# Flamingo gated block, one core: second output bank, earlier base weights, reordered K to Q change

## The chip, the cores and the metric

The kernel runs on one core of one Trainium2 chip. The metric is the device time of one execution in microseconds (us). Inputs are float32, and all matrix products are made from two-part splits: a value is rounded to a high part (a ScalarE copy to the fp32r type), the low part is value minus high part, and three matmuls (high by low, low by high, high by high) are summed. This is why nearly every operand passes ScalarE ("hi") and then VectorE or GpSimd ("lo") before TensorE may use it.

## What is computed

```python
# x (8,128,512), ctx (8,128,512), 32 heads of 128, mask per (batch, key)
def xattn(h):                                    # h = layernorm(x)
    q = (rmsnorm(h, ln_weight) @ w_q.T)          # (8,128,32*128)
    k, v = ctx @ w_k.T, ctx @ w_v.T
    s = softmax(where(m, q.k + position_bias, -inf)); s = where(m, s, 0)
    return h + (s @ v) @ w_out.T
def ffn(y):                                      # y = layernorm(x)
    base = y @ base_W.T + base_b                 # 512 x 512
    w = top-8 of softmax(y @ router_W.T + router_b), summed per expert by expert_map
    return base + 2 * sum_e w_e * (y @ A_e.T) @ B_e.T
x = x + tanh(g_xattn) * xattn(layernorm(x))
x = x + tanh(g_ffn) * ffn(layernorm(x))
```

## The kernel before

The program is written out by hand, one instruction stream per engine, with semaphores between them. It has three stages.

**K and Q.** 32 jobs (`JOBS`), job n for a pair of heads: jobs 0 to 15 make K from the context, jobs 16 to 31 make Q from the normalised x. `G` is 16, the number of the first Q job. From job 2 on, each job is a block-wise product with seven block multiplications m1 to m7 in place of eight (a Strassen-Winograd scheme). TensorE's order in a job is m1, m2, m4 of the job before, m6, m3 of the job before, m5, m7. The results R11, R21, R12, R22 are combined on VectorE (`c11`, `c12`, `c22`), rounded on ScalarE (`c11_hi`, `c21_hi`, ...), split on VectorE (`unit_lo`) and stored to `qk_units` in HBM. ScalarE also keeps copies of partial results (`snapshot_1` to `snapshot_3`, which write U1 to U3), on which m6, m7 and m4 wait. The weights of the next job are summed on VectorE (`weight_sums`, lines 930 to 935), rounded on ScalarE (`first_weights_hi`, `last_weights_hi`) and split on GpSimd. Beside this, jobs 3 to 13 normalise x (`layernorm_stats`, `rms_stats`, `norm_scales`, `normed`), and TensorE transposes it. At job 16 the four sums of x's blocks, T1 to T4, take the place of those of the context (`x_sum_hi`, `x_sum_lo`).

**Attention.** 64 units (`UNITS`): 8 groups of 4 heads by 8 batches. In step t each engine works on several units at once. TensorE: scores of unit t (line 1478), the two halves of V of unit t+1 (`v_half`), the two halves of the output product of unit t-4 (`out_half`), then probabilities times V of unit t-2 (`apply_probs`, line 1491). VectorE: adds the output of unit t-5 to `acc` (`add_out`, line 1082; in the last group `x1`, line 1095), V's low part, scores plus bias and mask and their maximum (lines 1048 to 1052), A's low part of unit t-3 (line 1056), then, when ScalarE has the exponentials (line 738), `rinv`, `rscale`, `p_norm` (lines 1060 to 1067) and a 32x32 block transpose (line 1073). SyncE sends the blocks to HBM (`p_rows`, line 333) and back transposed (`pT`, line 339), which ScalarE rounds two steps later (`probs_hi`) and GpSimd splits (`probs_lo`, line 516). GpSimd does four operations in a step: the rest of A (line 511), `probs_lo`, bias plus mask (line 504), and the low part of one weight tile.

**Last group and feed-forward.** In the last group (units 56 to 63) `x1`, the statistics and `y` of the second layernorm are added to VectorE's steps, and SyncE loads x again and the feed-forward weights. The base weights (`baseT`, 1 MB) go into the buffer `o_raw0`, which is free once output 55 is made (`o_done` at `LAST`). Then come the transposes of y, LoRA and router products, the base product and the result.

All outputs go to one PSUM bank, so an output waits for the sum of the one before it, which stands at the start of VectorE's step:

```python
# TensorE, out_half, first half
pe.wait_ge(a_lo_done, u + 1)
reached(pe, acc_done, u)          # last group: pe.wait_ge(f_x1, b)
# ScalarE, step, last group, ahead of exponentials(t)
if last and b >= 4:
    act.wait_ge(ld_base, 16)
    late_high(w_base_hi[:, b - 4, :], base_raw[:, b - 4, :])
```

## Time and profile before

| | |
|---|---|
| median of 3 runs | 892.32 us (890.05 to 893.9) |
| the profiled execution's own time | 891.21 us |
| its span, first to last instruction | 889.4 us |
| TensorE busy | 845.3 us (95%) |
| VectorE busy | 670.7 us (75%) |
| ScalarE, GpSimd busy | 499.1 us (56%), 487.3 us (55%) |
| mean granted TensorE clock | 0.984 |

The span is some 345 us of K and Q, some 455 us of attention up to the last group's units, and the rest. The busy shares are means over stages. A busy TensorE can still be one that follows another engine's pace with gaps of tenths of a microsecond, so the waits and the chain have to be read beside the shares. PE is TensorE, DVE is VectorE, ACT is ScalarE, POOL is GpSimd, SP is SyncE.

### The profile page before, as it was taken

Reading aid. Unit: us, or ns where it says so; the run is one execution under the profiler, and the core shown is the slowest. Engines: PE = TensorE matmul, PEld = TensorE weight load, DVE = VectorE, ACT = ScalarE, POOL = GpSimd, SP = SyncE. Lnnn points to the kernel's source line nnn. Section 1 sums busy time; section 2 is a strip of 40 time slices with the busy share of each in tenths; the row PEclk is TensorE's granted clock in tenths of the full one; section 3 lists DMA queues with packets and bytes.
Section 4 is the critical chain, followed back from the end, with each engine's and each line's share of the span. In section 5 each row is a group of like instructions: output and inputs, shape, how many; then the busy total and the mean of one; then the engine's idle time right before and its main releaser. Section 6 shows DMA issues by size and latency. Waiting matters only on the chain.

```text
span 889.4 us, 13885 instructions
## 1 busy us (share of the span) xinstructions
PE 845.3 (95%) x4204; PEld 706.6 (79%) x4204; DVE 670.7 (75%) x1174; ACT 499.1 (56%) x1185; POOL 487.3 (55%) x352
## 2 busy tenths in 40 slices
PE   6999999989999996999999999999999999977998
PEld 5877888768888884888888888888888888856786
DVE  6887777866766645888888888888888888859864
ACT  6556676666676643555555555655655555525310
POOL 0355334644466523666666666766666666646432
PEclk9999999999999998999999999999999999998999
DMA  8867677569877787889889898888888988974101
GB/s 289 307 238 284 258 263 280 205 261 356 301 272 279 274 314 236 249 242 259 235 239 259 239 256 248 249 261 244 241 255 250 253 252 248 272 214 133 46 25 71
DMA packets 155393, 214.73 MB, mean 241 GB/s; under 512 B 10960, under 2 KB 109392, under 8 KB 154960
## 3 DMA queue, kind: packets, MB, share of 16 engines
q1 hardware_dynamic: 155344, 214.13, 75.6%
q8 instruction: 24, 0.39, 0.2%
q14 instruction: 25, 0.20, 0.1%
HBM read 128.11 MB, written 85.98 MB: 241 GB/s over the span
## 4 chain that ended last, share of the span: by engine, by line
DVE 37%; PE 37%; ACT 12%; issue 7%; DMA 5%; DVEq 1%; SPq 1%; POOL 0%; ACTq 0%; POOLq 0%
ACT p_exp L738 10%; DVE p_norm L1067 6%; PE Sb L1331 5%; PE Sb L1333 5%; PE Sb L1332 5%; DVE s_sb L1050 4%; DVE negmax L1052 4%; DVE rscale L1062 4%; DVE V_lo L898 4%; DVE s_sb L1048 4%; DVE acc L1082 3%; PE Ab L1331 2%; PE Ab L1332 2%; PE Ab L1333 2%; DVE unit_out L898 2%
## 5 line engine op out<-in xcount | busy, mean ns | idle before, releaser
L467 POOL TENSOR_TENSOR w_lo<-w_raw,w_hi 128x1280 fp32r<-128x1280 f32 (+1 forms) x29 | 85.2, 2938 | 122.5 <-ACT w_hi L604 122.5
L511 POOL TENSOR_TENSOR a_rest<-small_a,A_hi 128x512 f32<-128x512 f32 x64 | 82.9, 1296 | 124.3 <-ACT small_a L732 124.2
L738 ACT ACTIVATE p_exp<-s_sb,negmax 128x128 f32<-128x128 f32 x256 | 99.8, 391 | 56.3 <-DVE negmax L1052 56.1
L1322 PE MATMUL Ob<-o_hi,A_lo 128*128 128x512 f32 x248 | 101.0, 407 | 17.5 <-DVE acc L1095 11.4
L516 POOL TENSOR_TENSOR P_hl<-pT,P_hl 128x512 fp32r<-128x512 f32 x64 | 83.0, 1297 | 39.5 <-ACT P_hl L604 39.0
L1323 PE MATMUL Ob<-o_lo,A_hi 128*128 128x512 f32 x248 | 98.2, 396 | 0.0
L1324 PE MATMUL Ob<-o_hi,A_hi 128*128 128x512 f32 x248 | 98.1, 396 | 0.0
L504 POOL TENSOR_TENSOR bm<-bias,maskneg 128x512 f32<-128x512 f32 x64 | 83.8, 1309 | 24.6 <-DVE s_sb L1048 24.6
L604 ACT ACTIVATE P_hl<-pT 128x512 fp32r<-128x512 f32 x64 | 40.5, 633 | 76.0 <-DMA pT<-p_rows 75.9
L604 ACT ACTIVATE U<-Sb 128x512 f32<-128x512 f32 x90 | 53.6, 599 | 47.1 <-PE Sb L1333 46.4
L604 ACT ACTIVATE A_hi<-Ab 128x512 fp32r<-128x512 f32 x64 | 38.4, 599 | 72.4 <-PE Ab L1492 72.4
L1322 PEld LDWEIGHTS Ob<-o_hi,A_lo 128*128 128x128 f32 x248 | 47.3, 191 | 38.4 <-issue 28.3
L604 ACT ACTIVATE w_hi<-w_raw 128x512 fp32r<-128x512 f32 (+2 forms) x67 | 60.1, 901 | 22.8 <-PE Kb L1333 7.3
L1060 DVE RECIPROCAL rinv<-rowsum 128x4 f32<-128x4 f32 x64 | 11.4, 178 | 80.8 <-ACT p_exp L738 80.8
L1331 PE MATMUL Sb<-t_hi,w_lo 128*128 128x512 f32 x180 | 70.3, 391 | 0.8 <-ACT U L604 0.7
L1491 PE MATMUL Ab<-P_hl,V_hi 128*128 128x256 f32 x256 | 63.7, 326 | 7.6 <-POOL P_hl L516 7.6
L1333 PE MATMUL Sb<-t_hi,w_hi 128*128 128x512 f32 x180 | 70.1, 389 | 0.0
L1332 PE MATMUL Sb<-t_lo,w_hi 128*128 128x512 f32 x180 | 70.0, 389 | 0.0
L1478 PE MATMUL Sb<-qk 128*128 128x256 f32 x256 | 66.4, 337 | 2.9 <-DVE s_sb L1050 2.2
L472 POOL TENSOR_TENSOR w_lo<-w_raw,w_hi 128x512 fp32r<-128x512 f32 x30 | 40.2, 1339 | 40.9 <-ACT w_hi L604 40.9
L898 DVE TENSOR_TENSOR unit_out<-Ob,unit_out 128x512 fp32r<-128x512 f32 x61 | 42.0, 689 | 23.7 <-ACT unit_out L604 23.0
L1491 PEld LDWEIGHTS Ab<-P_hl,V_hi 128*128 128x128 f32 x256 | 48.7, 190 | 11.1 <-POOL P_hl L516 8.7
(292 smaller groups left out, 2605.2 us busy)
## 6 DMA issues: line engine op xcount, KB each, us to landing
qk_units<-unit_out SPq DMA_DIRECT2D x128, 512.0 KB, 3.0
qk<-qk_units SPq DMA_DIRECT2D x64, 1024.0 KB, 7.2
p_rows<-p_blocks SPq DMA_DIRECT2D x64, 256.0 KB, 2.6
pT<-p_rows SPq DMA_DIRECT2D x256, 64.0 KB, 4.4
w_raw<-wqk SPq DMA_DIRECT2D x31, 512.0 KB, 4.3
v_raw<-wv SPq DMA_DIRECT2D x32, 256.0 KB, 4.8
o_raw<-wo SPq DMA_DIRECT2D x32, 256.0 KB, 5.0
stage<-ctxT SPq DMA_DIRECT2D x8, 256.0 KB, 6.2
```

Source lines behind the costliest of these rows:

```text
L467: pool.tensor_tensor(w_lo[:, n % 2, first:5, :], w_raw[:, n % 2, first:5, :], f32(w_hi[:, n % 2, first:5, :]), ALU.subtract).then_inc(w1_l ...
L504: pool.tensor_tensor(bm[:, :, :], bias4[:, q, :, :], maskneg[:, b:b + 1, :].broadcast_to([P, HU, S]), ALU.add).then_inc(bm_done, 1)
L604: act.activation(dst, src, ACT.Copy).then_inc(done, 1)
L738: last = act.activation(p_exp[:, i, :], s_sb[:, i, :], ACT.Exp, bias=negmax[:, i:i + 1], accum_out=rowsum[:, i:i + 1])
L898: dve.tensor_tensor(dst, src, f32(hi), ALU.subtract).then_inc(done, 1)
L1322: pe.matmul(dst, w_lo, m_hi, start=start, stop=False)
L1323: pe.matmul(dst, w_hi, m_lo, start=False, stop=False)
L1324: return pe.matmul(dst, w_hi, m_hi, start=False, stop=stop)
L1331: pe.matmul(bank, lo, m_hi[:, c, :], start=first, stop=False, skip_group_check=not fresh)
L1332: pe.matmul(bank, hi, m_lo[:, c, :], start=False, stop=False, skip_group_check=not fresh)
L1333: last = pe.matmul(bank, hi, m_hi[:, c, :], start=False, stop=c == 1, skip_group_check=not fresh)
L1491: pe.matmul(Ab[:, h, :, :], V_hi[:, r, h, :], P_hl[:, h, :, :], start=True, stop=False)
```

## The change

- Outputs of even batches go to `Ob`, of odd ones to `QP` (`o_bank`), so an output waits for the sum two before it. In the last group the banks are `Ob`, `QP`, `Ob`, `Vb`, `Ob`, `Vb`, `Ob`, `Vb`, and from the third batch on output b waits for `f_x1` at b-1 (the fourth for a V split instead). Two of the base product's banks are exchanged, and the first transpose of y waits for `f_x1` at 2.
- SyncE asks for the base weights at batch 3 of the last group instead of batch 4. ScalarE rounds three of their four tiles behind the exponentials of batches 5 to 7 and the fourth in the tail ahead of `probs_hi` of unit 62; GpSimd's splits follow (batches 5 to 7, and one in the tail).
- At job 16 VectorE makes R21's low part first, then R22's, then c11, and T4's low part behind it; ScalarE rounds R21 ahead of the next weights.
- x's statistics: the second half's four `bn_stats` are spread over jobs 4 to 7, its aggregates stand in job 7, its rms part in job 8 and its scale in job 9 (before: jobs 4, 5 and 6).
- Some semaphores are split: one for each weight tile of `wv` and `wo`, and one for each parity of the units for `pT`. No instruction is added by this.

The order of VectorE's instructions at job 16 (unit_out from Ob is R22's low part, from Sb R21's, from Vb R11's; lines 930 to 935 are the weight sums). Before, from the second sum of the weights:

```order
L935 TENSOR_TENSOR w_raw<-w_raw 128x256
L898 TENSOR_TENSOR t_lo<-stage,t_hi 128x1024
L898 TENSOR_TENSOR unit_out<-Ob,unit_out 128x4x128
L947 TENSOR_TENSOR Vb<-Ab,U 128x512
L898 TENSOR_TENSOR unit_out<-Vb,unit_out 128x4x128
L898 TENSOR_TENSOR unit_out<-Sb,unit_out 128x4x128
L959 TENSOR_TENSOR Ob<-Kb,U 128x512
```

Now (the code's lines have moved by 12):

```order
L947 TENSOR_TENSOR w_raw<-w_raw 128x256
L910 TENSOR_TENSOR unit_out<-Sb,unit_out 128x4x128
L910 TENSOR_TENSOR unit_out<-Ob,unit_out 128x4x128
L959 TENSOR_TENSOR Vb<-Ab,U 128x512
L910 TENSOR_TENSOR t_lo<-stage,t_hi 128x1024
L910 TENSOR_TENSOR unit_out<-Vb,unit_out 128x4x128
L971 TENSOR_TENSOR Ob<-Kb,U 128x512
```

The low part of R21 moved from the fifth place to the second, ahead of T4's low part (t_lo), and T4's now stands between c11 and R11's.

ScalarE in the last group, batch 4 before (o_hi from o_raw with ld_base is the first base tile):

```order
L604 ACTIVATE A_hi<-Ab 128x512 [waits o_done,pv_done]
L604 ACTIVATE V_hi<-Vb 128x512 [waits pv_done,v_done]
L732 ACTIVATE small_a<-Ab 128x512 [waits a_rest_done]
L604 ACTIVATE P_hl<-pT 128x4x128 [waits pv_done,pt_done]
L604 ACTIVATE o_hi<-o_raw 128x512 [waits ld_base]
L738 ACTIVATE p_exp,rowsum<-s_sb,negmax 128x128 [waits norm_done,max_done]
L738 ACTIVATE p_exp,rowsum<-s_sb,negmax 128x128 x3
```

Now, batch 5:

```order
L612 ACTIVATE A_hi<-Ab 128x512 [waits o_done,pv_done]
L612 ACTIVATE V_hi<-Kb 128x512 [waits pv_done,v_done]
L740 ACTIVATE small_a<-Ab 128x512 [waits a_rest_done]
L612 ACTIVATE P_hl<-pT 128x4x128 [waits pv_done,pt_done1]
L746 ACTIVATE p_exp,rowsum<-s_sb,negmax 128x128 [waits norm_done,max_done]
L746 ACTIVATE p_exp,rowsum<-s_sb,negmax 128x128 x3
L612 ACTIVATE o_hi<-o_raw 128x512 [waits ld_base]
```

The base tile moved from ahead of a unit's exponentials to behind those of the next unit.

SyncE's transfers in the last group, before, batches 3 end, 4 and 5 begin:

```order
L347 DMA qk<-qk_units 128x8x256 [waits scores_done]
L339 DMA pT<-p_rows 32x4x128 [waits rows_done]
L339 DMA pT<-p_rows 32x4x128 x3
L430 DMA x_again<-x 128x512 [waits f_u]
L433 DMA o_raw<-baseT 128x2048 [waits o_done]
L333 DMA p_rows<-p_blocks 128x512 [waits blocks_done]
L347 DMA qk<-qk_units 128x8x256 [waits scores_done]
L339 DMA pT<-p_rows 32x4x128 [waits rows_done]
```

Now:

```order
L346 DMA pT<-p_rows 32x4x128 [waits rows_done]
L346 DMA pT<-p_rows 32x4x128 x3
L437 DMA x_again<-x 128x512 [waits f_u]
L440 DMA o_raw<-baseT 128x2048 [waits o_done]
L340 DMA p_rows<-p_blocks 128x512 [waits blocks_done]
L354 DMA qk<-qk_units 128x8x256 [waits scores_done]
L346 DMA pT<-p_rows 32x4x128 [waits rows_done]
L346 DMA pT<-p_rows 32x4x128 x3
```

The base weights moved ahead by one round of probabilities, scores' operands and x.

The diff, without the semaphores that are split:

```diff
+        def o_bank(b):
+            return (Ob[:, :], QP[:, :])[b % 2]
...
-        out_bank = [Ob[:, :]] * 4 + [Vb[:, :], Ob[:, :], Vb[:, :], Ob[:, :]]
+        out_bank = [Ob[:, :], QP[:, :], Ob[:, :], Vb[:, :], Ob[:, :], Vb[:, :], Ob[:, :], Vb[:, :]]
...
-        base_bank = [flat(Ab)[:, 0:D], flat(Ab)[:, D:2 * D], Vb[:, :], Ob[:, :]]
+        base_bank = [flat(Ab)[:, 0:D], flat(Ab)[:, D:2 * D], Ob[:, :], Vb[:, :]]
...
-                    if last and b == 4:
+                    if last and b == 3:
                         sp.wait_ge(o_done, LAST)
                         sp.dma_start(base_raw[:, :, :], baseT).then_inc(ld_base, 16)
...
-                if last and b >= 4:
-                    late_low(b - 2, w_base_lo[:, b - 4, :], base_raw[:, b - 4, :], w_base_hi[:, b - 4, :])
+                if last and b >= 5:
+                    late_low(b - 3, w_base_lo[:, b - 5, :], base_raw[:, b - 5, :], w_base_hi[:, b - 5, :])
...
-                if n in (4, 5):
-                    rms_root(n - 4)
-                if n in (3, 4):
-                    layernorm_root(n - 3)
+                if n in (4, 8):
+                    rms_root(n // 8)
+                if n in (3, 7):
+                    layernorm_root(n // 7)
...
             late_root(3)
+            late_low(5, w_base_lo[:, 3, :], base_raw[:, 3, :], w_base_hi[:, 3, :])
             a_remainder(UNITS - 2, 0)
...
-                if last and b >= 4:
+                exponentials(t)
+                if last and b >= 5:
                     act.wait_ge(ld_base, 16)
-                    late_high(w_base_hi[:, b - 4, :], base_raw[:, b - 4, :])
-                exponentials(t)
+                    late_high(w_base_hi[:, b - 5, :], base_raw[:, b - 5, :])
...
+                if n == G:
+                    c21_hi(n - 1)
                 if n + 1 < JOBS:
                     first_weights_hi(n + 1)
...
-                if n > PLAIN:
+                if n > PLAIN and n != G:
                     c21_hi(n - 1)
...
             y_hi(0)
-            probs_hi(UNITS - 2, 0)
+            late_high(w_base_hi[:, 3, :], base_raw[:, 3, :])
+            probs_hi(UNITS - 2, 0, UNITS // 2)
...
-                dve.tensor_tensor(acc[:, b, :], Ob[:, :], acc[:, b, :], ALU.add).then_inc(acc_done, 1)
+                dve.tensor_tensor(acc[:, b, :], o_bank(b), acc[:, b, :], ALU.add).then_inc(acc_done, 1)
...
                 if n == G:
-                    x_sum_lo(T4)
+                    unit_lo(R21, n - 1, X[(n - 1) % 2])
                 if n > PLAIN:
                     unit_lo(R22, n - 1, C22)
                 c11(n)
+                if n == G:
+                    x_sum_lo(T4)
                 unit_lo(R11, n, C11)
-                if n > PLAIN:
+                if n > PLAIN and n != G:
                     unit_lo(R21, n - 1, X[(n - 1) % 2])
...
                 if n == 4:
                     rms_stats(0)
-                    layernorm_stats(1)
+                    tile_stats(1, 0)
                 if n == 5:
                     norm_scales(0)
+                if 5 <= n < 8:
+                    tile_stats(1, n - 4)
+                if n == 7:
+                    layernorm_stats(1)
+                if n == 8:
                     rms_stats(1)
-                if n == 6:
+                if n == 9:
                     norm_scales(1)
...
-                    if late and b == 4:
+                    if isinstance(u, int) and u == 1:
+                        pe.wait_ge(v_lo_done, 2)
+                    if late and b == 3:
                         pe.wait_ge(v_lo_done, UNITS - 1)
-                    elif late and b > 4:
+                    elif late and b > 1:
                         pe.wait_ge(f_x1, b - 1)
-                    elif late and b > 0:
-                        pe.wait_ge(f_x1, b)
                     else:
-                        reached(pe, acc_done, u)
+                        reached(pe, acc_done, u - 1)
...
-                if j < 2:
-                    pe.wait_ge(v_lo_done, UNITS if j == 1 else 2)
+                if j == 0:
+                    pe.wait_ge(f_x1, 2)
+                elif j == 1:
+                    pe.wait_ge(v_lo_done, UNITS)
                 else:
```

## Rows read from the trace of the kernel before

**Rows 1.** The page's chain of waits, by engine.

```profile
DVE 37%; PE 37%; ACT 12%; issue 7%; DMA 5%; DVEq 1%; SPq 1%; POOL 0%; ACTq 0%; POOLq 0%
```

**Rows 2.** The chain in order of time, one unit of attention: start us, us, what.

```profile
402.07 0.65 DVE acc L1082
...
405.39 1.66 ACT p_exp L738 x8
...
410.10 0.65 DVE acc L1082
```

**Rows 3.** VectorE's lines between 371 and 792 us: ns min/median/max, first and last start.

```profile
L1082 DVE TENSOR_TENSOR acc<-Ob,acc x56: 650/652/654, 372.2 to 786.3; 128x512 f32<-128x512 f32 x56
...
L1062 DVE TENSOR_TENSOR rscale<-rinv,valid x55: 161/590/1258, 377.4 to 784.7; 128x4 f32<-128x4 f32 x55
...
L1067 DVE TENSOR_TENSOR p_norm<-p_exp,rscale x56: 691/692/1737, 370.8 to 784.9; 128x512 f32<-128x512 f32 x56
```

**Rows 4.** Waits between 371 and 792 us: us in total, times, longest.

```profile
PE Ob L1322 <- DVE acc L1082: 5.4, 12, 1.3
```

**Rows 5.** Timeline, TensorE: start us, us, instruction [idle before it <-releaser].

```profile
785.36 0.33 PE L1478 MATMUL Sb<-qk 128*128 128x256 f32 x1
...
792.68 0.33 PE L1478 MATMUL Sb<-qk 128*128 128x256 f32 x1
...
803.44 0.76 PE L1322 MATMUL Ob<-o_hi,A_lo 128*128 128x512 f32 x1 [8.23 <-DVE acc L1095]
...
832.46 0.36 PE L1491 MATMUL Ab<-P_hl,V_hi 128*128 128x256 f32 x1 [0.73 <-POOL P_hl L516]
```

**Rows 6.** Timeline, last group: SyncE's transfers, ScalarE, VectorE, GpSimd.

```profile
786.38 0.34 SPq L333 DMA_DIRECT2D p_rows<-p_blocks  x1
...
791.58 0.43 SPq L433 DMA_DIRECT2D o_raw<-baseT  x1
...
788.21 0.63 ACT L604 ACTIVATE P_hl<-pT 128x512 fp32r<-128x512 f32 x1 [1.07 <-DMA pT<-p_rows]
798.61 0.63 ACT L604 ACTIVATE o_hi<-o_raw 128x512 fp32r<-128x512 f32 x1 [9.77 <-DMA o_raw<-baseT]
...
825.25 0.40 ACT L738 ACTIVATE p_exp<-s_sb,negmax 128x128 f32<-128x128 f32 x1 [5.12 <-DVE negmax L1052]
...
828.51 0.60 ACT L604 ACTIVATE A_hi<-Ab 128x512 fp32r<-128x512 f32 x1 [1.61 <-PE Ab L1492]
...
788.88 0.69 DVE L1052 TENSOR_REDUCE negmax<-s_sb 128x4 f32<-128x512 f32 x1
...
802.58 0.71 DVE L1095 SCALAR_TENSOR_TENSOR acc<-Ob,tgate,acc 128x512 f32<-128x512 f32 x1
...
830.98 1.28 POOL L516 TENSOR_TENSOR P_hl<-pT,P_hl 128x512 fp32r<-128x512 f32 x1
```

**Rows 7.** Transfers by line: KB each, median us from issue to landing.

```profile
p_rows<-p_blocks SPq DMA_DIRECT2D x64, 256.0 KB, 2.6
pT<-p_rows SPq DMA_DIRECT2D x256, 64.0 KB, 4.4
...
o_raw<-baseT SPq DMA_DIRECT2D x1, 1024.0 KB, 7.0
```

**Rows 8.** Timeline, K to Q change: TensorE, then VectorE, then ScalarE.

```profile
182.19 0.77 PE L1331 MATMUL Sb<-x_hi,w_lo 128*128 128x512 f32 x1 [4.10 <-DVE unit_out L898]
...
186.54 0.39 PE L1331 MATMUL Sb<-t_hi,w_lo 128*128 128x512 f32 x1
...
177.66 1.22 DVE L898 TENSOR_TENSOR t_lo<-stage,t_hi 128x1024 fp32r<-128x1024 f32 x1
...
183.17 0.59 ACT L604 ACTIVATE U<-Sb 128x512 f32<-128x512 f32 x1
```

**Rows 9.** Stretches: us, busy us of PE, PEld, DVE, ACT, POOL, then PEclk, DMA share, GB/s.

```profile
60.00:70.00 10.00, 8.62 (x40) 6.79 (x39) 8.09 (x17) 6.68 (x12) 6.44 (x5) 1.00 0.72 262
182.00:185.50 3.50, 3.31 (x8) 2.67 (x9) 2.70 (x7) 1.46 (x3) 1.07 (x1) 0.51 0.93 371
```

34 lines of the change are left out of this document (19 added, 15 removed).

## Prediction

> **What bounds the kernel now.** I read the page's shares first: TensorE 95% busy, VectorE 75%. That would make it a TensorE kernel. The chain of waits says otherwise: VectorE holds as much of it as TensorE (37% each) and ScalarE 12% [rows 1]. The chain in order of time shows where. In attention it runs from VectorE's sum into `acc` through its scores and maximum to ScalarE's exponentials (1.66 us) and back to VectorE, round and round, with no TensorE row in it; one such round took 410.10 - 402.07 = 8.03 us [rows 2]. So I took the pace: 56 sums into `acc` start from 372.2 to 786.3 us, which is 7.53 us a unit [rows 3]. TensorE, when nothing holds it, needs 792.68 - 785.36 = 7.32 [rows 5]. It follows. VectorE's round is long because two operations with both inputs in SBUF, `rscale` and `p_norm`, run between 161 and 1258 ns, and between 691 and 1737 ns [rows 3], with GpSimd at work beside them.
>
> Three places stand out against that pace. In batch 4 of the last group ScalarE waits 9.77 us for the base weights ahead of the exponentials, and TensorE's next output waits 8.23 us behind it [rows 5, 6]. At the K to Q change TensorE waits 4.10 us for VectorE [rows 8]. In the normalisation of x, TensorE is busy 8.62 us of 10 between 60 and 70 us [rows 9].
>
> **The base weights.** They are asked for at 791.58 us and ScalarE gets on at 798.61 [rows 6]. The transfer takes 7.0 us [rows 7]. Asked for a round earlier it is issued when output 55 is made, just ahead of step 60 at 785.36 [rows 5], 6 us earlier, and the first user is a unit later and behind its exponentials. Nobody waits for it. What is late next in batch 4 is VectorE's maximum (788.88 + 0.69 = 789.6; ScalarE is free at 788.8), so the exponentials start at 789.6 where they started some 0.5 after 798.61, at 799.2: 9.6 us. I take 0.4 off for `p_norm`, which then meets GpSimd; a meeting costs from 0 to 1737 - 691 = 1046 ns [rows 3]. x1 of batch 0 moves from 802.58 to 793.4 [rows 6], 9.2 earlier.
>
> From there to the end of the steps VectorE is the bound, and its shift holds. The exponentials of unit 63 come at 825.25 - 9.2 = 816.05 and end at 817.7. Before, ScalarE then waited 1.61 us for TensorE, which had been held by x1 [rows 6]; with its output bank free TensorE is early, and this wait goes. Ahead of the probabilities of unit 62 stand five conversions, two of them the moved base tiles, at 0.5 us from start to start (my estimate: they take 0.60 to 0.63 each and overlap a little [rows 6]), then 0.63 for itself: 820.8. GpSimd's split takes 1.28 [rows 6], so TensorE's product of unit 62 starts at 822.1 where it was 832.46 [rows 5]: 10.3 us. Behind it the tail is TensorE's own work nearly throughout, and the shift holds. The last base split on GpSimd (about 1.3 us) falls between a root and a wait for ScalarE; if that cover is gone it costs up to 1.3.
>
> The 1 MB is now under way when `p_rows` of unit 59 is issued (786.38), which takes 2.6 us by itself, and `pT` 4.4 [rows 6, 7]. Bounds: 0, if the earlier request only fills gaps; 4, if all of the probabilities of unit 59 stand behind it (the rival below). I take 0.5, nearer to 0, because they are read a step later. **Term: -9.8 us.**
>
> **The K to Q change.** R21's low part takes T4's place at 177.66 and is done at 178.3, so m1 of job 17 starts at 178.5 in place of 182.19. After m1 and m2 (2.7 us, below) m4 of job 16 wants to start at 181.2, but needs U3, which ScalarE ended at 183.17 + 0.59 [rows 8]. That copy follows c12, and only gains the 0.7 us in which VectorE waited between c11 and R11's split, now filled by T4. So m4 starts at 183.0 in place of 186.54 [rows 8]: -3.5 us, with an idle of 0.5 and one of 1.9 left. The granted clock was 0.51 in the 3.5 us from 182 us, after the idle of 4.10 us [rows 8, 9]; that is the level of 1.2 GHz. TensorE was busy 3.31 us of it, which would have been half at 2.4 GHz, so 1.65 us of the loss was clock, and m1 and m2, 186.54 - 182.19 = 4.35, need 2.7 at full rate. Bounds: -2.0, if it falls again after the smaller idles; -5.8, if U3 does not hold m4. **Term: -3.5 us.**
>
> **x's statistics.** The 1.38 us that TensorE loses there [rows 9] are two gaps of about the same length: one behind the four `bn_stats` and four aggregates of the second half, which goes, and one ahead of the first transpose, which still waits for the same operations. The aggregates land in jobs 7 and 8; VectorE was busy 8.09 us of 10 in this stretch [rows 9] and has room. **Term: -0.7 us**, between 0 and -1.4.
>
> **The two banks.** Removed is the wait of an output for the sum before it: 5.4 us in 12 waits [rows 4]. Against 7.32 a unit, TensorE is even (7.53 - 7.32) x 55 = 11.5 us over. I cost it at nothing. VectorE never waits for TensorE here, so a TensorE that runs further ahead changes no round; its waits come back at the next thing VectorE or the transfers give, the probabilities of unit t-2, some 0.6 us further on. Bounds: 0 and -11.5. In the last group the bank matters for the third and fourth output; that is in the 10.3. No added wait holds anything: the fourth output waits for the V split of unit 62, made a step before; output 60 needs x1 of batch 2, made at the start of step 63, ahead of A's low part for which it waits anyway.
>
> **Split semaphores** cost nothing: no instruction is added, and each wait is for the same data.
>
> **Sum**: -9.8 - 3.5 - 0.7 = -14.0. The profiled execution took 891.21 us (span 889.4), so 877.2. The median of the runs, 892.32, is 1.1 above it, and the runs spread over 3.9; I say 877.5.
>
> **Rivals.**
>
> *A, the two banks free attention.* If TensorE's lateness did reach VectorE, through the time at which GpSimd starts (it takes A's rest once TensorE's product is rounded), the pace falls towards 7.32 and up to 11.5 us more go: 866. For it: TensorE's outputs wait there 12 times. Against it: the chain has no TensorE row. 0.10.
>
> *B, the base weights hold the probabilities.* If transfers of a queue go one behind the other, 1 MB at the 262 to 371 GB/s of the stretches [rows 9] takes 2.8 to 4.0 us. `p_rows` then lands at 786.38 + 2.6 + 4.0 = 793, and `pT` 4.4 behind it, with its four issues at 797.4 to 799; ScalarE reads it ahead of exponentials that could start a round after 789.6, near 797.6, and GpSimd and TensorE follow. Cost 2 to 4: 880.5. For it: ScalarE waited for `pT` already 1.07 us in batch 4 [rows 6]. Against: the loads of scores' operands, as large, pass there in each round. 0.22. By the Trainium skill (DMA: Bandwidth & Descriptors, Queues, rings and completion order) descriptors are consumed in ring order on each DMA engine, which speaks for B; no row here shows the order.
>
> *C, slower: GpSimd meets VectorE in every unit.* TensorE ahead starts `a_rest` earlier, and so moves GpSimd's four operations against `rscale` and `p_norm`. In the worst rounds these cost 1.1 us more than their least (1258 - 161 [rows 3]), in the mean 0.6: the round of 8.03 had the 1.1 in it, 6.93 without, and the mean is 7.53. Were the worst to come in all 55 units, that is +0.5 x 55 = +27, net 905; it decides from +0.25 a unit on, a mean cost of 0.85. Against it: GpSimd's run starts with the probabilities, which come by transfers that VectorE paces, not TensorE. 0.03. The Trainium skill (SBUF — State Buffer, Who interferes with whom) has an exclusive lock between VectorE's operations with two SBUF inputs and GpSimd's; the spread there [rows 3] agrees. By it a shift of phase can turn the cost of a unit either way.
>
> *D, the K to Q change gains little*: the clock falls again and U3 holds m4, -2.0 or less; 879 with all else. 0.12.
>
> *E, nothing comes of it*: the wait of 9.77 us is replaced by one as long, say for scores' operands, whose load shares the queue. 887 to 890. 0.05.
>
> **How the numbers follow.** My forecast has 0.48, A 0.10, B 0.22, D 0.12, E 0.05, C 0.03. The range has to hold 8 in 10: B and D lie in it, half of A's way, and the run's own spread. 870 to 884. About 0.5% is what a measurement here can tell from no change, 4.5 us: faster means below 887.9. All but C and most of E are below: 0.92; within 0.5%: 0.05; slower: 0.03.
>
> **What the profile after would show.** Right: ScalarE's wait for `baseT` gone; TensorE without a wait over 3 us between 780 and 815; sums into `acc` still 7.5 us apart, and TensorE's waits in attention now at the probabilities (line of `P_hl`) instead of at the output; at 178 us an idle under 1 us and one near 2, for ScalarE's copy; full granted clock at both places. Wrong: a pace of 7.3 or of over 7.7 us in attention (A, C); a wait of ScalarE of over 3 us for `pT` in batch 5 (B); or a half clock after the small idles (D). The forecast falls if VectorE's steps in batches 5 to 7, where it is busy all the time, are longer than before.

## The result, and the profile after

The changed kernel takes 880.33 us (median of 4 runs, 876.11 to 884.0) where the kernel before takes 892.62 (4 runs). The ratio is 0.9856, with a 95% interval of 0.9814 to 0.9898. That is 12.9 us less, and between 9.1 and 16.6. The profiled execution was the slowest of the four, 884.0 us, span 882.1; its difference to the span before, 7.3 us, is smaller than the one between the medians. The table further down shows where these 7.3 us lie.

The page's chain of waits after, by engine (before: [rows 1]):

```profile
DVE 40%; PE 34%; ACT 12%; issue 7%; DMA 5%; SPq 1%; DVEq 1%; POOL 0%; ACTq 0%
```

VectorE's lines in attention after, 371 to 786 us (ns min/median/max, first and last start), against [rows 3]:

```profile
L1095 DVE TENSOR_TENSOR acc<-QP,acc x28: 650/652/654, 377.6 to 785.5; 128x512 f32<-128x512 f32 x28
...
L1075 DVE TENSOR_TENSOR rscale<-rinv,valid x55: 161/697/1312, 375.2 to 784.0; 128x4 f32<-128x4 f32 x55
L1080 DVE TENSOR_TENSOR p_norm<-p_exp,rscale x55: 691/692/1750, 376.3 to 784.2; 128x512 f32<-128x512 f32 x55
```

From the sum of output 1 (377.63) to that of output 55 (785.52) it is 407.9 us, 7.55 a unit: the pace is the old one, and `rscale` stalls as it did. Only the place of TensorE's waits has changed, from the output [rows 4] to the product with the probabilities, two thirds of it for A's low part and one third for the probabilities themselves (waits, TensorE, 371 to 786 us: us in total, times, longest):

```profile
PE Ab L1513 <- DVE A_lo L1069: 3.8, 9, 0.6
PE Ab L1513 <- POOL P_hl L523: 1.9, 4, 0.7
```

The K to Q change after, timeline: VectorE, then ScalarE, then TensorE, against [rows 8]:

```profile
177.53 0.68 DVE L910 TENSOR_TENSOR unit_out<-Sb,unit_out 128x512 fp32r<-128x512 f32 x1
...
182.76 1.08 ACT L612 ACTIVATE U<-Sb 128x512 f32<-128x512 f32 x2
...
178.36 0.47 PE L1353 MATMUL Sb<-x_hi,w_lo 128*128 128x512 f32 x1 [0.41 <-DVE unit_out L910]
...
183.50 0.47 PE L1353 MATMUL Sb<-t_hi,w_lo 128*128 128x512 f32 x1 [2.16 <-ACT U L612]
```

m1 of job 17 starts at 178.36 in place of 182.19, m4 of job 16 at 183.50 in place of 186.54, with the two idles that were forecast, 0.41 and 2.16. The windows that answer to [rows 9]:

```profile
60.00:70.00 10.00, 9.92 (x47) 7.98 (x46) 8.50 (x14) 6.02 (x10) 4.25 (x2) 1.00 0.68 257
182.00:185.50 3.50, 2.00 (x9) 1.71 (x10) 2.67 (x7) 2.18 (x4) 0.16 (x1) 1.00 0.87 349
```

The clock stays at full speed here, and the two gaps in the normalisation of x are gone, both of them. One of 0.39 us stands 10 us further on, ahead of the second tile's transposes, where there was none before:

```profile
78.16 0.66 PE L1447 MATMUL QP<-ident,xn 128*128 128x128 f32 x4 [0.39 <-DVE xn L1010]
```

The last group after: SyncE's transfers, ScalarE's waits, VectorE's first x1, and all that TensorE waits for from 780 us to product 63 ([rows 5, 6] before):

```profile
778.85 0.34 SPq L340 DMA_DIRECT2D p_rows<-p_blocks  x1
...
781.12 1.75 SPq L346 DMA_DIRECT2D pT<-p_rows  x4
...
783.38 0.43 SPq L440 DMA_DIRECT2D o_raw<-baseT  x1
785.63 0.33 SPq L340 DMA_DIRECT2D p_rows<-p_blocks  x1
...
791.34 2.75 SPq L346 DMA_DIRECT2D pT<-p_rows  x4
...
795.63 0.63 ACT L612 ACTIVATE P_hl<-pT 128x512 fp32r<-128x512 f32 x1 [2.67 <-DMA pT<-p_rows]
797.15 0.40 ACT L746 ACTIVATE p_exp<-s_sb,negmax 128x128 f32<-128x128 f32 x1 [0.88 <-DVE negmax L1065]
...
816.01 0.40 ACT L746 ACTIVATE p_exp<-s_sb,negmax 128x128 f32<-128x128 f32 x1 [3.79 <-DVE negmax L1065]
...
792.62 0.71 DVE L1108 SCALAR_TENSOR_TENSOR acc<-Ob,tgate,acc 128x512 f32<-128x512 f32 x1
...
782.89 0.36 PE L1513 MATMUL Ab<-P_hl,V_hi 128*128 128x256 f32 x1 [0.64 <-DVE A_lo L1069]
797.96 0.35 PE L1513 MATMUL Ab<-P_hl,V_hi 128*128 128x256 f32 x1 [0.17 <-issue]
808.16 0.55 PE L1513 MATMUL Ab<-P_hl,V_hi 128*128 128x256 f32 x1 [2.65 <-DVE A_lo L1069]
816.84 0.35 PE L1513 MATMUL Ab<-P_hl,V_hi 128*128 128x256 f32 x1 [0.41 <-DVE A_lo L1069]
823.49 0.36 PE L1513 MATMUL Ab<-P_hl,V_hi 128*128 128x256 f32 x1 [2.29 <-DVE A_lo L1069]
835.08 0.39 PE L1513 MATMUL Ab<-P_hl,V_hi 128*128 128x256 f32 x1 [1.25 <-POOL P_hl L523]
```

ScalarE no longer waits for `baseT`, and TensorE's idle of 8.23 us is gone. In its place stand waits for A's low part, 2.65 and 2.29 us, and these cost more than their length (windows of the same columns as [rows 9]; the first two after, the last two before):

```profile
808.00:811.50 3.50, 3.34 (x16) 3.37 (x16) 2.94 (x7) 2.87 (x10) 1.68 (x1) 0.50 0.22 70
824.90:827.90 3.00, 3.00 (x16) 2.90 (x15) 2.90 (x8) 1.01 (x3) 1.94 (x2) 0.50 0.02 5
...
800.00:806.60 6.60, 3.16 (x8) 2.52 (x9) 5.51 (x12) 3.26 (x10) 4.50 (x5) 0.50 0.40 106
820.40:827.10 6.70, 5.51 (x14) 4.28 (x15) 6.07 (x12) 1.65 (x8) 3.31 (x4) 0.50 0.35 111
```

The granted clock is 0.50, 1.2 GHz, right behind each of them. The kernel before was at 0.50 twice in this group too, around its idles of 8.23 us and, ahead of an output at 821.59, of 3.17 us. Product 63 came 11.59 us after product 62, where it took 9.94 before, though the waits ahead of product 63 are the same (1.24 and 1.25).

**Where the time went, stretch by stretch.** The landmarks are starts in the profiled execution of each kernel: VectorE's c11 (`Vb<-Ab,U`) of its first, 14th and last occurrence, the sums of outputs 1 and 55, TensorE's product of unit 63 (its first matmul), the end of the span. Every stretch is the difference of two starts, in us. The experiments' rows are here too.

| kernel | to first c11 | to 14th c11 | to last c11 | to sum 1 | to sum 55 | to product 63 | to the end |
|---|---|---|---|---|---|---|---|
| before | 34.9 | 129.0 | 156.6 | 59.4 | 406.4 | 56.1 | 47.0 |
| changed | 35.3 | 128.4 | 153.8 | 60.2 | 407.9 | 49.6 | 47.0 |
| e1 base weights only | 35.2 | 128.9 | 156.7 | 59.3 | 410.5 | 48.6 | 47.0 |
| e2 K to Q only | 33.9 | 129.0 | 153.8 | 59.4 | 411.0 | 59.5 | 48.6 |
| e3 banks only | 35.9 | 128.9 | 157.2 | 59.2 | 408.5 | 55.6 | 48.6 |
| e4 one bank | 34.5 | 128.4 | 155.4 | 60.2 | 408.7 | 48.4 | 47.0 |
| e5 changed again | 34.6 | 128.3 | 153.8 | 59.6 | 404.3 | 52.0 | 48.6 |
| e6 request late | 34.6 | 128.4 | 153.8 | 58.8 | 408.1 | 48.2 | 47.1 |
| e7 splits ahead | 34.8 | 128.4 | 153.7 | 58.8 | 408.9 | 49.2 | 48.6 |
| e8 scalar norm | 35.7 | 128.4 | 155.4 | 61.6 | 412.7 | 55.5 | 48.6 |
| e9 GpSimd's order | 34.2 | 128.4 | 153.8 | 57.4 | 397.1 | 50.9 | 47.1 |
| e10 GpSimd's order, one bank | 34.7 | 128.3 | 153.8 | 58.4 | 397.1 | 48.6 | 47.0 |
| e11 one bank again | 34.7 | 128.4 | 153.8 | 59.2 | 406.0 | 48.5 | 48.6 |
| e12 statistics behind | 34.6 | 128.3 | 153.7 | 58.2 | 397.2 | 46.4 | 47.1 |

Between the two profiled executions: +0.4 at the start, -0.6, -2.8, +0.8, +1.5, -6.5, 0.0, in sum -7.3 with rounding. The three that have to do with the change are the x statistics, the K to Q order and the last group, -9.9 together. The start (33.9 to 35.9) and attention (404.3 to 411.0 for kernels that don't differ in what bounds it) move by 2 and by 6.7 us from one execution to the next. So does the last group: with the base weights as before, the last two columns come to 103.1, 108.1 and 104.3 (before, e2, e3).

### The profile page after: what moved, and what is told of

The parts are those of the page before. It is cut to its first block, busy times and chain, and to the rows that moved or that the text cites. A ratio compares the mean times of both kernels' runs of the same rounds, so it can differ in the third digit from the quotient of the medians.

```text
span 882.1 us, 13849 instructions
## 1 busy us (share of the span) xinstructions
PE 844.8 (96%) x4204; PEld 707.1 (80%) x4204; DVE 675.5 (77%) x1174; ACT 499.0 (57%) x1185; POOL 489.1 (55%) x352
## 4 chain that ended last, share of the span: by engine, by line
DVE 40%; PE 34%; ACT 12%; issue 7%; DMA 5%; SPq 1%; DVEq 1%; POOL 0%; ACTq 0%
ACT p_exp L746 10%; DVE p_norm L1080 5%; PE Sb L1353 5%; PE Sb L1355 4%; PE Sb L1354 4%; DVE s_sb L1063 4%; DVE rscale L1075 4%; DVE negmax L1065 4%; DVE s_sb L1061 4%; DVE V_lo L910 4%; DVE acc L1095 3%; DMA pT<-p_rows 2%; PE Ab L1353 2%; PE Ab L1355 2%; PE Ab L1354 2%
## 5 line engine op out<-in xcount | busy, mean ns | idle before, releaser
L511 POOL TENSOR_TENSOR bm<-bias,maskneg 128x512 f32<-128x512 f32 x64 | 83.1, 1299 | 24.3 <-DVE s_sb L1061 24.3
L1513 PE MATMUL Ab<-P_hl,V_hi 128*128 128x256 f32 x256 | 66.5, 337 | 20.4 <-POOL P_hl L523 10.7
L612 ACT ACTIVATE w_hi<-w_raw 128x512 fp32r<-128x512 f32 (+2 forms) x67 | 60.2, 903 | 22.7 <-PE Kb L1355 6.9
L612 ACT ACTIVATE A_hi<-Ab 128x512 fp32r<-128x512 f32 x64 | 38.3, 598 | 39.4 <-PE Ab L1514 39.3
L1502 PE MATMUL Sb<-qk 128*128 128x128 f32 x256 | 57.9, 226 | 0.0
L1514 PE MATMUL Ab<-P_hl,V_lo 128*128 128x128 f32 x256 | 57.6, 225 | 0.0
L612 ACT ACTIVATE unit_out<-Ob 128x512 fp32r<-128x512 f32 x61 | 36.4, 597 | 35.8 <-DVE Ob L971 27.9
L1086 DVE STREAM_TRANSPOSE p_blocks<-p_norm 128x512 f32<-128x512 f32 x64 | 45.5, 712 | 10.2 <-DVE p_norm L1080 9.6
```

What stands on the lines that cost most here:

```text
L511: pool.tensor_tensor(bm[:, :, :], bias4[:, q, :, :], maskneg[:, b:b + 1, :].broadcast_to([P, HU, S]), ALU.add).then_inc(bm_done, 1)
L612: act.activation(dst, src, ACT.Copy).then_inc(done, 1)
L1513: pe.matmul(Ab[:, h, :, :], V_hi[:, r, h, :], P_hl[:, h, :, :], start=True, stop=False)
```

## The experiments

Ratios are to the kernel before, run on the same chip, with their 95% interval.

**e1_base_only.** The kernel before with, of the change, only the request at batch 3 and the conversions and splits behind the exponentials.

```diff
-                    if last and b == 4:
+                    if last and b == 3:
                         sp.wait_ge(o_done, LAST)
...
-                if last and b >= 4:
+                exponentials(t)
+                if last and b >= 5:
                     act.wait_ge(ld_base, 16)
-                    late_high(w_base_hi[:, b - 4, :], base_raw[:, b - 4, :])
-                exponentials(t)
+                    late_high(w_base_hi[:, b - 5, :], base_raw[:, b - 5, :])
```

> The kernel before with the base weights alone moved (asked for at batch 3, conversions and splits behind the exponentials), one output bank. Theory: ScalarE's wait of 9.77 us is the whole loss there, the bank plays a small part. In the changed kernel's trace this part, measured from VectorE's step at 786 us to TensorE's product of unit 62, came to 8.2 us, and 1.7 us of it was lost again before the product of unit 63. With one bank TensorE still waits for the sums at the start of VectorE's steps, which costs some 1 to 2 us of it: 6 to 8 us less than before, 884.5 to 886.5. Rival (the bank carries it): under 4 us less, above 888.5, with TensorE waiting over 3 us in all for sums into acc in batches 4 to 7.

Measured: 887.52 us, ratio 0.9927 (0.9898 to 0.9956), that is -6.5 us (-3.9 to -9.1). The stretch from sum 55 to product 63 is 48.6 us in place of 56.1. So this part carries the last group alone, at one bank. The median is 1 us above the range of the theory and 1 below that of the rival. The rival's sign did come, TensorE's waits for the sums there are 0.25 and 3.64 us, but not its price: the wait for A's low part ahead of product 62 is 2.01 us, so the group is as short as with two banks.

**e2_kq_only.** The kernel before with the K to Q order alone (VectorE's R21 first, T4 behind c11, `c21_hi` ahead of the next weights).

> The kernel before with the K to Q order alone. Theory: the start of m4 of job 16 moves from 186.5 to 183.5 us and everything behind it with it: 3.0 us less, 889.6. Rival (attention gives it back, because VectorE's round takes another phase against GpSimd): 0 to 1 us less, 891.6 to 892.6, with the 3 us seen at 186 us and gone at 755 us.

Measured: 893.14 us, ratio 0.9982 (0.9951 to 1.0012). The total tells nothing apart: its interval, -4.4 to +1.1 us, holds the theory and the rival. The stretch does: 153.8 us in place of 156.6, 156.7 and 157.2 in the three executions without it. Attention took 411.0 us in this one, and the last group 59.5, neither of which this part touches. The rival, that attention gives the 3 us back, isn't borne out by the other executions that have it, 404.3 to 408.9.

**e3_banks_only.** The kernel before with the two banks alone.

```diff
-                        reached(pe, acc_done, u)
+                        reached(pe, acc_done, u - 1)
...
-product(out_bank[b] if late else Ob[:, :], ...
+product(out_bank[b] if late else o_bank(b), ...
```

> The kernel before with the two output banks alone. Theory: VectorE's round sets the pace of attention, so the pace stays at 7.53 us a unit and TensorE's waits move from the output to the probabilities. ScalarE still waits for the base weights, with TensorE one output further on, which shortens TensorE's idle without moving the end by more than 1 us: 891.5 to 892.6, no difference that can be measured. Rival (A of the prediction): 11 us less, 881.5, pace 7.32.

Measured: 895.73 us, ratio 1.0019 (0.9992 to 1.0046): no difference. Attention took 408.5 us. The last group of this execution shows the wait for the base weights undiminished, and TensorE one output further on behind it (timeline, ScalarE and TensorE):

```profile
802.37 0.63 ACT L607 ACTIVATE o_hi<-o_raw 128x512 fp32r<-128x512 f32 x1 [9.88 <-DMA o_raw<-baseT]
...
811.68 0.55 PE L1494 MATMUL Ab<-P_hl,V_hi 128*128 128x256 f32 x1 [9.75 <-DVE A_lo L1059]
```

**e4_one_bank and e11_one_bank_again.** The changed kernel with the banks undone, twice.

> The changed kernel with the banks undone: one output bank, the old waits. Theory: 0 to 2 us more than the changed kernel's 880.3, so 880.3 to 882.5, the cost being in batches 5 to 7 of the last group, where an output waits for x1. Rival A: 11 us more, 891. Rival (the banks cost something, by a shift of GpSimd against VectorE): less than 880.3.

> The changed kernel with one bank a second time. Its ratio to the kernel before was 0.9908 (0.9873 to 0.9944), that of the changed kernel 0.9856 and 0.9818, on other chips. Paces of single executions: one bank 7.500, 7.605, 7.622, 7.590; two banks 7.534, 7.543, 7.482, 7.529, 7.558. Theory (banks are worth nothing in attention): ratio near 0.983, as the changed kernel's. Rival (the banks are worth 0.05 us a unit, 3 us in all): ratio near 0.988 and a pace of 7.57 or more.

Measured: 885.17 us, ratio 0.9908 (0.9873 to 0.9944), and 882.82 us, ratio 0.9849 (0.9799 to 0.9899). The first is 2.7 us above its expected range and alone would have told for the banks (the changed kernel has 0.9856); 1.6 us of it stand in the K to Q stretch, where the clock fell in this execution. The second lies between its theory and its rival. On the same chip the changed kernel has 0.9818 (e5); the intervals overlap, and the medians differ by 1.5 us. Attention took 408.7 and 406.0 us, inside the spread of the two-bank kernels (404.3 to 408.9). TensorE does wait at the output again (waits of e4, 371 to 786 us), and the attention stretch is none the longer:

```profile
PE Ob L1344 <- DVE acc L1095: 6.8, 17, 1.0
```

**e5_changed_again.** The changed kernel, unaltered.

> The changed kernel itself, on the chip of the other runs of this set. It shows how far the pace of attention differs between two executions of one kernel: before and the four variants so far had 7.50 to 7.62 us a unit over 50 units, with no order by what they change. Theory (the spread is VectorE's meetings with GpSimd, which fall differently each time): a pace anywhere between 7.50 and 7.62, and a time between 879 and 886. Rival (the two banks set the pace): again 7.53, and a time within 1 us of 880.3.

Measured: 881.33 us (878.98 to 883.03), ratio 0.9818 (0.9783 to 0.9852). Attention took 404.3 us, 7.49 a unit (just under the theory's range, and not the 7.53 of the rival), where the first execution had 407.9, so one kernel's own spread is at least 3.6 us there. The collision behind it can be read row by row in this trace (GpSimd, then VectorE):

```profile
499.72 1.28 POOL L502 TENSOR_TENSOR o_lo<-o_raw,o_hi 128x512 fp32r<-128x512 f32 x1
502.02 1.30 POOL L518 TENSOR_TENSOR a_rest<-small_a,A_hi 128x512 f32<-128x512 f32 x1 [1.02 <-ACT small_a L740]
504.47 1.29 POOL L523 TENSOR_TENSOR P_hl<-pT,P_hl 128x512 fp32r<-128x512 f32 x1 [1.15 <-ACT P_hl L612]
505.71 1.29 POOL L511 TENSOR_TENSOR bm<-bias,maskneg 128x512 f32<-128x512 f32 x1
506.96 1.30 POOL L502 TENSOR_TENSOR o_lo<-o_raw,o_hi 128x512 fp32r<-128x512 f32 x1
...
500.25 0.77 DVE L1075 TENSOR_TENSOR rscale<-rinv,valid 128x4 f32<-128x4 f32 x1
501.05 0.69 DVE L1080 TENSOR_TENSOR p_norm<-p_exp,rscale 128x512 f32<-128x512 f32 x1
...
507.81 0.47 DVE L1075 TENSOR_TENSOR rscale<-rinv,valid 128x4 f32<-128x4 f32 x1
```

`rscale`, four elements a partition, ends at 501.02, and the GpSimd operation that was under way when it came ends at 501.00: a weight tile's low part (L502), the last of the four in a step. In the next unit the bias and mask (L511) runs from 505.71 to 507.00 and the weight tile from 506.96 to 508.26, and `rscale` ends at 508.28. It is a 128x4 operation that waits for the end of a 128x512 one. Of the 54 `rscale` between the sums of outputs 1 and 55 of this execution, 43 end within 0.04 us of the end of a weight tile's low part on GpSimd, and nine take under 0.2 us. After such a wait `p_norm` runs at once, in 0.69. This led to e9.

**e6_request_late.** The changed kernel with the request at batch 4 again (`b == 3` back to `b == 4`), conversions left behind the exponentials.

> The changed kernel with the base weights asked for at batch 4 again, and their conversions left behind the exponentials. Theory (the place behind the exponentials does the work, and the place of the request little): issued near 794.6 us, landed near 801.6, first user behind the exponentials of unit 61 at 798.8, so ScalarE waits some 3 us where it then waits for the probabilities anyway; 0 to 1 us more than the changed kernel. The probabilities of unit 59 land 3 us sooner than in the changed kernel, without effect. Rival (the request does it): 3 us more or worse.

Measured: 881.09 us, ratio 0.9826 (0.9791 to 0.986), the same as e5 on the same chip. The request was issued at 789.45 (not at 794.6, since it is ahead of `p_rows` and not behind it). ScalarE has no wait for `baseT` at all: its first conversion starts at 797.29, 7.8 us behind the request, where the transfer took 7.0 in the kernel before. To product 63 it took 48.2 us. So the earlier request wasn't needed once the conversions stood behind the exponentials.

**e7_splits_ahead.** The reverse: the request left at batch 3, the conversions and splits where they were before.

> The changed kernel with the base weights' conversions ahead of the exponentials of batches 4 to 7 again, the request left at batch 3. Theory: issued at 783.4, landed at 790.4 or later, first user at 788.1; ScalarE waits 2 to 3 us and the exponentials start 2.5 to 3.5 us later, and the four conversions of 0.6 stand ahead of exponentials in batches 5 to 7, 1.8 more: 3 to 5 us more than the changed kernel. Rival (VectorE's chain hides it, or the request was all): under 1 us more.

Measured: 884.88 us, ratio 0.9876 (0.9839 to 0.9914), 3.6 us over e5. ScalarE waits for the weights, now 2.30 us:

```profile
790.04 0.63 ACT L611 ACTIVATE o_hi<-o_raw 128x512 fp32r<-128x512 f32 x1 [2.30 <-DMA o_raw<-baseT]
```

x1 of batch 0 starts 9.4 us after sum 55 (7.1 in the changed kernel), product 62 comes 39.3 after it (38.0 in the changed kernel, 38.8 in e5), product 63 at 49.2 (49.6 and 52.0). So between 0.4 and 1.3 us of the 3.6 are placed, at product 62; product 63 comes no later, because the clock fell for less time here, and the rest was not located. Each of the two halves of this part is enough to remove most of the 9.77 us. By the totals the place behind the exponentials is the better one (all six runs of e7 lie above all six of e5 and of e6).

**e8_scalar_norm.** The changed kernel with `rscale` left out and `p_norm` in four operations.

```diff
-                dve.tensor_tensor(rscale[:, :], rinv[:, :], valid[:, b:b + 1].broadcast_to([P, HU]),
-                                  ALU.mult).then_inc(rscale_done, 1)
...
-                dve.tensor_tensor(p_norm[:, :, :], p_exp[:, :, :], scale, ALU.mult).then_inc(norm_done, 1)
+                for h in range(HU):
+                    ins = dve.tensor_scalar(p_norm[:, h, :], p_exp[:, h, :], rinv[:, h:h + 1], valid[:, b:b + 1],
+                                            ALU.mult, ALU.mult)
+                ins.then_inc(norm_done, 1)
```

> The changed kernel with rscale left out and p_norm made by four operations with two scalar operands for each partition (1/sum, valid), 128 columns each, in place of one of 512 with two inputs in SBUF. The result is the same. Theory (VectorE's round with its meetings of GpSimd bounds attention): rscale and p_norm took 0.62 + 0.81 = 1.43 us in the mean, four operations of about 0.2 take 0.8 and meet GpSimd less; the round falls under TensorE's 7.32 and TensorE becomes the bound: pace 7.3, 10 us less than the changed kernel, 870. Rival 1 (each of the four waits for GpSimd instead): pace 7.5 or more, no gain. Rival 2 (attention is bound by TensorE or by transfers after all): the round's VectorE work shrinks and the pace stays.

Measured: 897.59 us, ratio 1.0003 (0.9969 to 1.0036), 16 us over e5, of which 8.4 in attention by the two profiled executions. Rival 1's outcome came true, its reason in part. The group of the four (371 to 765 us):

```profile
L1077 DVE TENSOR_SCALAR p_norm<-p_exp,rinv,valid x204: 330/339/1497, 377.3 to 761.3; 128x128 f32<-128x128 f32 x102
```

One takes 330 ns at least and not 200, so four take 1.3 us before any wait. They are held up too, up to 1497 ns; the mean of one is 458, 1.8 us for four, where `rscale` and `p_norm` took 0.68 + 0.79 in the mean (after, 371 to 786 us). Attention took 412.7 us, 7.64 a unit. The theory of the round wasn't tested by this, for the round did not get shorter.

**e9_gpsimd_order.** The changed kernel with the weight tile's low part moved in GpSimd's step from the last place to the one behind the rest of A, a step later (so that ScalarE has its high part by then).

```diff
                     a_remainder(t - 3, (b - 3) % 2)
+                if b <= 1 and not first:
+                    split_wo_lo(g, q, 2 + b)
+                if not last and 2 <= b <= 5:
+                    split_wv_lo(g + 1, 1 - q, b - 2)
+                if not last and b >= 6:
+                    split_wo_lo(g + 1, 1 - q, b - 6)
...
                 if b == 0 and not first:
-                    split_wo_lo(g, q, 3)
-                if not last and 1 <= b <= 4:
-                    split_wv_lo(g + 1, 1 - q, b - 1)
-                if not last and b >= 5:
-                    split_wo_lo(g + 1, 1 - q, b - 5)
+                    pass
```

> The changed kernel with one GpSimd operation moved in each step of attention: the low part of a weight tile (1.3 us), which stood last and was under way when rscale came (o_lo from 499.72 to 501.00 us, rscale from 500.25 to 501.02), stands between the rest of A and the split of the probabilities, one step later, where GpSimd was idle 0.5 to 2.2 us. Theory (VectorE's round with its meetings of GpSimd bounds attention): rscale falls to 0.16 and p_norm stays at 0.69 in most units, the round to 6.95, and TensorE's 7.32 becomes the bound: pace 7.32 to 7.35, 10 to 12 us less than the changed kernel, 869 to 871. Rival (the meetings only move, to the bias and mask ahead or to the rest of A behind): pace 7.5, no gain. Rival (the split of the probabilities comes too late): TensorE waits for it in each unit, pace over 7.55.

Measured: 872.16 us, ratio 0.9737 (0.969 to 0.9783). Against e5's 0.9818 that is some 7 us less, by the medians 9. (The pair with one bank, e10 and e11, ran together on one chip: 870.91 and 882.82, 12 us.) Attention: 397.1 us, 7.35 a unit, where the ten executions with the old order and the old `p_norm` took 404.3 to 411.0. GpSimd and VectorE in one unit:

```profile
499.22 1.30 POOL L518 TENSOR_TENSOR a_rest<-small_a,A_hi 128x512 f32<-128x512 f32 x1 [2.27 <-ACT small_a L742]
500.48 1.30 POOL L502 TENSOR_TENSOR o_lo<-o_raw,o_hi 128x512 fp32r<-128x512 f32 x1
501.74 1.29 POOL L523 TENSOR_TENSOR P_hl<-pT,P_hl 128x512 fp32r<-128x512 f32 x1
502.99 1.28 POOL L511 TENSOR_TENSOR bm<-bias,maskneg 128x512 f32<-128x512 f32 x1
...
503.76 0.52 DVE L1077 TENSOR_TENSOR rscale<-rinv,valid 128x4 f32<-128x4 f32 x1
504.32 0.69 DVE L1082 TENSOR_TENSOR p_norm<-p_exp,rscale 128x512 f32<-128x512 f32 x1
```

`rscale` now waits for the bias and mask, to 504.27, and doesn't fall to 0.16 as the theory had it. But it takes about the same half microsecond in most units (50 of 54 end within 0.04 us of the end of the bias and mask, and the median is 0.53 us), for the order of GpSimd's operations no longer lets a fourth one run on into it, and `p_norm` takes 0.71 in the mean. TensorE's waits between 371 and 765 us are down to one:

```profile
PE Ab L1515 <- DVE A_lo L1071: 0.2, 1, 0.2
```

So TensorE is the bound now: 7.35 a unit against the 7.32 of [rows 5].

**e10_gpsimd_order_one_bank.** The same with one output bank.

> As the run before, with one output bank. Theory: once VectorE's round is shorter than TensorE's, an output's wait for the sum before it is TensorE's own loss: pace 7.4 to 7.6, 3 to 12 us more than with two banks. So the banks, worth little while VectorE bounds, are worth something here. Rival (the banks never matter): the same time as with two banks, within 1 us.

Measured: 870.91 us, ratio 0.9718 (0.967 to 0.9765), 1.3 us under e9 by the medians. The rival holds: attention 397.1 us again, and between 371 and 765 us TensorE waits once for the sum:

```profile
PE Ob L1346 <- DVE acc L1097: 1.4, 1, 1.4
```

Where TensorE is the bound it is late at its output, and the sum has long been made. Where VectorE is the bound, the wait is at the output or at the next thing. In neither case did a second bank gain anything that these runs can tell; the 3 to 12 us of the theory are ruled out.

**e12_stats_behind.** e10 with x1's statistics in batches 5 to 7 moved behind A's low part.

```diff
                     x1(b - 5)
-                    x1_stats(b - 5)
...
                     x_plus_gated(b - 1)
+                if last and b >= 5:
+                    x1_stats(b - 5)
                 normalise(t, b)
```

> The kernel of the run with GpSimd's order changed and one output bank, with the statistics of x1 (1.05 us in three operations) moved in batches 5 to 7 of the last group from ahead of V's low part to behind the sum of x and the gated part, where VectorE waits 0.4 us for the exponentials. Theory (behind the base weights VectorE is what TensorE waits for: A's low part, 2.0 us ahead of the product of unit 62, and x1, 2.1 and 2.2 us ahead of two outputs): the scores and A's low part come 1 us sooner, the round is 0.4 us shorter in each of three units; from VectorE's sum of output 55 to TensorE's product of unit 63 it took 48.6 us and takes 46.5 to 47.5; 1 to 2 us less in all, ratio to the kernel before 0.970. Rival (the exponentials come sooner too and then wait for the statistics behind them, so the round only shifts): 48.6, no change.

Measured: 869.88 us, ratio 0.9721 (0.9694 to 0.9748); no difference from e10 in the ratio. In the trace the stretch to product 63 is 46.4 us, where e10 has 48.6, e11 48.5 and e4 48.4, and TensorE's wait ahead of product 62 is 1.29 in place of 1.99:

```profile
808.39 0.36 PE L1516 MATMUL Ab<-P_hl,V_hi 128*128 128x256 f32 x1 [1.29 <-DVE A_lo L1071]
```

This is 2.2 us in one execution, at its place and just over the size expected; it is not shown by the total. e10 and e12 are the shortest versions of this study, some 25 us under the kernel before (0.9718 and 0.9721; e12 by its interval 22 to 27).

## Why the prediction was right, and where its steps were off

The forecast was 877.5 with a range of 870 to 884. Measured: 880.33. The places were the right ones, the banks were worth nothing as forecast, and the sum of -14.0 was somewhat high. That the total came within 3 us is in part luck: the three terms, as the two profiled executions show them, come to -9.9.

**Base weights: -9.8 forecast.** Measured alone -6.5 us (e1); by the stretches to product 63 and to the end, 103.1 before against 95.6, 95.4, 97.1 and 95.7 with one bank (e1, e4, e11, e10), -7.2 in the mean; 96.6 and 100.6 in the changed kernel. The 103.1 is one execution; against e2, which has the last group as before and took 108.1, it would be -12. The total of e1 rests on 12 runs and is the firmer figure. The first half of the step was exact: x1 of batch 0 moved by 9.2 (from 16.3 to 7.1 us behind sum 55), and unit 63's exponentials came at 816.01, forecast 816.05 (the group began 0.75 us sooner in this execution, so counted from sum 55 they are 0.7 late). The step that failed is the next: "GpSimd's split takes 1.28, so TensorE's product of unit 62 starts at 822.1". It started at 823.49, 2.1 us late counted from sum 55, and not GpSimd held it but VectorE, whose A_lo stands behind y, x1, its statistics and y's low part (after, VectorE and GpSimd; then VectorE before):

```profile
822.55 0.68 DVE L1069 TENSOR_TENSOR A_lo<-Ab,a_rest 128x512 fp32r<-128x512 f32 x1
...
821.35 1.26 POOL L523 TENSOR_TENSOR P_hl<-pT,P_hl 128x512 fp32r<-128x512 f32 x1
...
831.52 0.68 DVE L1056 TENSOR_TENSOR A_lo<-Ab,a_rest 128x512 fp32r<-128x512 f32 x1
```

A_lo ends at 823.23, GpSimd's split at 822.61. Before, the two ended at 832.20 and 832.26 [rows 6]: A_lo was level with the split already and could move only by VectorE's shift of about 9, so the 10.3 us of the working were out of reach. Counted from sum 55 the product gained 8.2. VectorE was right to be called the bound up to the end of the steps; its hold reached one product further. The second loss wasn't in the working at all: the clock fell behind the wait of 2.29 us, 1.65 us more (3.2 in e5 and e9, behind a wait of 2.28). "TensorE without a wait over 3 us" came true, "full granted clock at both places" only for K to Q.

The prediction gave both the earlier request and the later conversions as the reason that nobody waits. Either does most of it (e6, e7), and by e6 the request could have stayed at batch 4.

**K to Q: -3.5 forecast, -2.8 measured** (153.8 against 156.6 to 157.2). The starts of m1 (178.36, forecast 178.5) and the idles 0.41 and 2.16 (0.5 and 1.9) are as worked out; ScalarE's copy for m4 gained 0.4 us (from 183.17 to 182.76) of the 0.7 that the working gave it, so m4 came at 183.50 for 183.0. Rival D is half true: in two of the eleven executions with this order (e4 and e8), the stretch took 155.4, with the clock at half behind the idle of 2.14 us in e4 and of 2.18 in e8. In e4:

```profile
182.70:186.20 3.50, 3.49 (x9) 2.76 (x10) 3.33 (x8) 2.23 (x3) 0.11 (x1) 0.52 1.04 349
```

**x's statistics: -0.7 forecast, -0.6 measured** (128.4 against 129.0; 128.3 to 128.5 in all ten executions with this part and 128.9 to 129.0 in the four without; no run has it alone). The way there was another: both gaps went, 1.3 us by the windows (9.92 busy for 8.62), 0.39 came back ahead of the second tile's transposes, where `xn` took 1.58 us in place of 0.74, and some 0.4 was not located. "One ahead of the first transpose, which still waits for the same operations" was wrong, and the sum came right by luck.

**The two banks: 0 forecast, none measured** (e3 1.0019 with an interval of 0.9992 to 1.0046; e11 with 0.9849 against 0.9818, intervals that overlap; e10 with 0.9718 against e9's 0.9737). Rival A, 11 us, is refuted; a microsecond or two in the total, either way, these runs can't tell. In the last group they may even cost a little: with them the stretch to product 63 took 49.6, 52.0 and 50.9 us (changed, e5, e9), without them 48.6, 48.4, 48.5 and 48.6 (e1, e4, e11, e10). In the first three TensorE's idle lies in two waits for A_lo, about 23 and 38 us behind sum 55, and the clock fell behind both; with one bank it lies partly at the outputs, and the clock fell once. e6 has two banks and 48.2, with one fall, so it is the clock that costs, and the banks only by where they put the idle. No total shows it.

**Rival B: mechanism seen, no price.** With the base weights ahead of it, `p_rows` of unit 59 (785.63) let `pT` go 5.7 us later, where the unit before took 2.3, and the same unit in the kernel before 2.9 (786.38 [rows 6] to this row of its SyncE timeline):

```profile
789.31 1.75 SPq L339 DMA_DIRECT2D pT<-p_rows  x4
```

In the changed kernel ScalarE waited 2.67 us for these probabilities. But the exponentials behind started by VectorE's maximum, 0.88 us later still. The 0.5 us that I set aside were not seen. The other runs bear the mechanism out: in the ten executions in which the base weights were issued just ahead of unit 59's `p_rows`, its `pT` went 5.6 to 6.3 us later, and in the three with the old request 2.9 to 3.2. In e6, where they were issued between the `p_rows` of units 59 and 60, it was 3.5 us for unit 59 and 5.7 for unit 60. By the Trainium skill (DMA: Bandwidth & Descriptors, Queues, rings and completion order) descriptors are consumed in ring order on each DMA engine; the delay of about 3 us agrees.

**Rival C** didn't occur in this change: 7.49 and 7.55 a unit. But its object, GpSimd's phase against VectorE, turned out to be the largest lever here, in the other direction (e9). By the Trainium skill (SBUF — State Buffer, Who interferes with whom) a VectorE operation with two SBUF inputs and a GpSimd one that reads SBUF lock each other out; e5's and e9's rows agree to 0.02 us. It is shown that taking one GpSimd operation out of the way takes 7 to 14 us out of attention and leaves TensorE the bound.

What stays open: the total moved by 12.9 us (9.1 to 16.6), the three places by about 10. The difference between the two is within the interval and within what attention and the last group spread by themselves; no further effect was looked for.

## What to carry to other kernels

Where two engines take turns on a path that a third one follows, as here, a buffer for the third gained nothing; ask first whose wait ends last. With the conversions behind the work that the critical path needed, the moment of the request no longer mattered (e6). When a wait goes, look for an engine that was ready at nearly the same moment: here A_lo, 0.06 us ahead of the split that was seen to hold TensorE. And when the same operation runs between 0.16 and 1.3 us in one trace, look which operation of the other engine ends at the moment at which it ends: here its place in a list of four was worth 7 to 12 us, as much as the largest part of the change or more.

## What the runs showed of the hardware

- A VectorE operation of four elements with two SBUF inputs (`rscale`) took 161 to 1312 ns, and ended within 0.02 us of the end of GpSimd's 128x512 operation (501.02 and 501.00).
- A VectorE multiplication by two scalar operands of 128 columns of float32 took at least 330 ns; one of 512 columns with two tensor inputs takes 691.
- TensorE's clock fell to 1.2 GHz in some executions and not in others behind the same idle at the same place: behind the one of 2.14 to 2.18 us at the K to Q change it was 1.00 in nine executions and about half in two (e4, e8). Behind the last idle, of 1.25 us ahead of product 63, the tail took 47.0 or 47.1 us in eight executions, with the clock at 1.00, and 48.6 in six (e2, e3, e5, e7, e8, e11), in each of which it fell to 0.50, beginning 0.2 to 1.3 us behind the start of product 63. The end of such a fall in e5:

```profile
835.00:838.00 3.00, 3.00 (x10) 2.34 (x10) 0.69 (x1) 0.00 (x0) 1.26 (x1) 0.63 0.00 0
```

- The attention stretch took 404.3 to 411.0 us in ten executions with the old GpSimd order (without e8), and 397.1, 397.1 and 397.2 in the three with the new. The spread of the whole kernel did not shrink with it: the six runs of e10 lie between 868.75 and 877.01 and those of e12 between 866.75 and 874.94, those of e5 and e6 within 4.1 and 3.1 us.
